# An audio tower on one core: two scale-and-add steps leave VectorE for ScalarE and GpSimd, and every engine's order is written anew

## The reference, cut to what matters

```python
h = tok(x)                                        # 32 x 626 x 128: frames of 128 samples times a DCT basis
h = h + mamba_both_ways(layernorm(h))             # L0_attn
h = h + experts(layernorm(h))                     # L0_ffn: 8 experts, the best 2 for each token
h = h + attention(layernorm(h))                   # L1_attn
h = h + patterns(layernorm(h))                    # L1_ffn: top 64 of 512, top 128 of 256, top 64 of 512

# in L0_attn, for each direction: y is the scan's output, gated
y = y * silu(z)
y = y * rsqrt(mean(y * y, -1) + EPS) * normw
y @ Wout.T                                        # both directions are projected, added to x and normalised
# in L0_ffn
combined = einsum('td,te->td', expert_out, gate_output)     # two experts' answers, each times its weight
```

## Time and profile before

| | |
|---|---|
| median of 3 runs | 8031.15 us (7994.39 to 8032.64) |
| profiled execution, its own time | 8044.3 us |
| its span, first to last instruction | 8042.4 us |
| mean granted TensorE clock | 0.867 of full speed |
| busy: PE, DVE, ACT, POOL | 76%, 84%, 45%, 31% |

### The profile page before, as it was taken

One profiled execution on the slowest core, in us unless ns is written; L12 is line 12 of the kernel. 1 busy time (PEld: TensorE's weight loads), 2 busy tenths in 40 slices (PEclk: granted clock), 3 DMA queues, 4 the chain that ended last, 5 costly groups with the idle time before them and its releaser, 6 DMA issues.

```text
span 8042.4 us, 115198 instructions
## 1 busy us (share of the span) xinstructions
PE 6126.0 (76%) x34088; PEld 4811.3 (60%) x34088; DVE 6747.5 (84%) x21836; ACT 3593.5 (45%) x7726; POOL 2468.3 (31%) x2872
## 2 busy tenths in 40 slices
PE   6777787877787777777777778777778777778643
PEld 5656666656666656666656666666666666666422
DVE  2368889888888888889888889888988888888897
ACT  2344445444445444445444445444445444445321
POOL 2233332233332233332233332323332333332220
PEclk8888898888888888898888899888889888889766
DMA  2322222222222222222222222221222222222200
GB/s 71 112 72 67 67 86 78 66 68 67 67 86 78 66 69 65 66 86 79 65 72 65 66 84 79 72 71 59 66 82 79 75 69 63 64 81 80 68 6 4
DMA packets 342571, 560.36 MB, mean 70 GB/s; under 512 B 33728, under 2 KB 261792, under 8 KB 341664
## 3 DMA queue, kind: packets, MB, share of 16 engines
q10 hardware_dynamic: 152576, 357.68, 14.1%
q1 hardware_dynamic: 168992, 153.83, 7.0%
q0 software_dynamic: 20480, 41.98, 1.8%
HBM read 484.63 MB, written 68.74 MB: 69 GB/s over the span
## 4 chain that ended last, share of the span: by engine, by line
PE 36%; DVE 27%; ACT 15%; issue 10%; POOL 6%; ACTq 4%; DMA 2%; POOLq 0%; DVEq 0%; SPq 0%
DVE m L1230 6%; PE pM L656 6%; PE pS L547 5%; PE pM L667 4%; PE pA L709 4%; DVE work L1233 3%; POOL rows L449 3%; DVE sorted L1260 2%; DVE work L1263 2%; ACT hid L915 2%; DVE a L1233 2%; ACTq L895 2%; PE pS L609 2%; PE pS L601 2%; PE pA L721 2%
## 5 line engine op out<-in xcount | busy, mean ns | idle before, releaser
L1230 DVE MAX8 m<-work 128x8 f32<-128x512 f32 x1792 | 1143.6, 680 | 1.0
L547 PE MATMUL pS<-u_fm,wconv_s 128*128 128x315 f32 x3072 | 1015.0, 485 | 94.1 <-ACT xs L860 87.0
L1233 DVE MATCH_REPLACE8 work<-m,work 128x512 f32<-128x512 f32 x1536 | 1026.6, 676 | 0.0
L656 PE MATMUL pM<-turned,expert 128*128 128x128 f32 x4352 | 675.3, 304 | 409.5 <-ACT turned L928 399.2
L410 POOL TENSOR_TENSOR yg<-xs,zs 128x525 f32<-128x525 f32 (+1 forms) x256 | 195.9, 797 | 2489.8 <-ACT xs L870 2489.8
L656 PEld LDWEIGHTS pM<-turned,expert 128*128 128x128 f32 x4352 | 606.2, 213 | 522.5 <-issue 492.5
L547 PEld LDWEIGHTS pS<-u_fm,wconv_s 128*128 128x128 f32 x3072 | 654.0, 217 | 404.6 <-issue 128.3
L915 ACT ACTIVATE hid<-pM,expert 128x128 f32<-128x128 f32 x2176 | 623.2, 372 | 250.5 <-PE pM L656 249.0
L1230 DVE MAX8 m<-a 128x8 f32<-128x512 f32 x768 | 505.4, 679 | 187.9 <-issue 180.9
L667 PE MATMUL pM<-expert,hid 128*128 128x128 f32 x4352 | 629.1, 292 | 0.0
L1263 DVE MATCH_REPLACE8 work<-sorted,work 128x128 f32<-128x128 f32 x2240 | 591.6, 276 | 0.0
(11 more groups left out here) (255 smaller groups left out, 14526.7 us busy)
## 6 DMA issues: line engine op xcount, KB each, us to landing
expert<-in_experts ACTq DMA_DIRECT2D x544, 578.0 KB, 4.0
ab<-decay_rows SPq DMA_DIRECT2D x384, 230.7 KB
rows<-routed_rows SPq DMA_DIRECT2D x128, 256.0 KB, 3.6
answer_rows<-turned ACTq DMA_DIRECT2D x256, 128.0 KB, 3.9
x_sb<-in_x SPq DMA_DIRECT2D x32, 256.0 KB
out<-hk SPq DMA_DIRECT2D x32, 256.0 KB
routed_rows<-un,slot POOLq DMA_INDIRECT x320, 2.2
rows<-answer_rows,slot POOLq DMA_INDIRECT x320, 2.6
```

Source lines behind the costliest of these rows:

```text
L547: last = nc.tensor.matmul(pS[:, 512 * (n % 3):512 * (n % 3) + HQ], wt, tap(d, i, half * HQ, HQ), start=(j == 0), stop=(j == len(blocks) - 1))
L656: last = nc.tensor.matmul(pM[:, bank(i) + j * P:bank(i) + (j + 1) * P], w1_of(i, j), turned[:, (i + 2) % 4, 1, :], start=True, stop=True)
L1230: link(nc.vector.max(m8[:, i, :], now[i]), len(tiles) - 1)
L1233: link(nc.vector.match_replace(work[i], m8[:, i, :], now[i], GONE), len(tiles) - 1)
```

## The change

Two pieces of VectorE's work are done elsewhere, and the five order strings are new.

- The scaled scan outputs. Ten instructions on DVE (multiply and add) become ten on ACT (a copy out of PSUM with a scale for each partition, into the first half of `zs4`, `dir_out`) and two adds of 128x640 on POOL.
- The experts' answers. Ten instructions on DVE become ten on ACT (scaling `rows` in place, `scaled`) and two adds of 128x640 on POOL (`h3_part`, `moe_done`).

```diff
-    o_ps=1, ub=1, r_norm=1, attn_scaled=2, h1_done=1,
+    o_ps=1, ub=3, dir_out=1, r_norm=1, attn_scaled=2, h1_done=1,
...
-DVE_ORDER = ("342414424142141142444444444414414444141114111441111111411114111414444444341444414444444344344344342")
+DVE_ORDER = ("44432414422141211444444444444434444411144114314434444134444111131111411111114441144444144444444441")
...
@@ pool_stage1
+            pool.wait_ge(G["dir_out"].s, G["dir_out"](b, 1))
+            for d in range(2):
+                pool.wait_ge(G["ub"].s, G["ub"](b, d + 1))
+                nc.gpsimd.tensor_tensor(ub[:], ub[:], zs4[:, d, 0, :].rearrange("p (t d) -> p t d", t=TILES), ALU.add).then_inc(G["ub"].s, 1)
+            yield
             normalized(pool, 0, 3, b, u, ub).then_inc(G["r_norm"].s, 1)
...
@@ pool_stage2
+            pool.wait_ge(G["scaled"].s, G["scaled"](b, 1))
+            pool.wait_ge(G["h3_kept"].s, G["h3_kept"](b, 0))
+            pool.wait_ge(G["u4_done"].s, G["u4_done"](b, 0))
+            nc.gpsimd.tensor_tensor(h3[:], h2[:], rows[:, 0:TILES, :], ALU.add).then_inc(G["h3_part"].s, 1)
+            pool.wait_ge(G["h3_part"].s, G["h3_part"](b, 1))
+            nc.gpsimd.tensor_tensor(h3[:], h3[:], rows[:, TILES:, :], ALU.add).then_inc(G["moe_done"].s, 1)
...
@@ act_stage1
+            act.wait_ge(G["o_ps"].s, G["o_ps"](b, 1))
+            act.wait_ge(G["rstd1"].s, G["rstd1"](b, 2))
+            for k in range(2 * TILES):
+                d, t = divmod(k, TILES)
+                last = nc.scalar.activation(zs4[:, d, 0, tok(t)], pS[:, tok(k)], ACT.Copy, scale=rstd[0][:, k:k + 1])
+            last.then_inc(G["dir_out"].s, 1)
...
@@ act_stage2
+            act.wait_ge(gathered.s, gathered(b, 160))
+            for k in range(2 * TILES):
+                last = nc.scalar.activation(rows[:, k, :], rows[:, k, :], ACT.Copy, scale=top8[:, k % TILES, k // TILES:k // TILES + 1])
+            last.then_inc(G["scaled"].s, 1)
...
@@ dve_stage1
-            for d in range(2):
-                for t in range(TILES):
-                    k = d * TILES + t
-                    last = nc.vector.scalar_tensor_tensor(ub[:, t, :], pS[:, tok(k)], rstd[0][:, k:k + 1], ub[:, t, :], ALU.mult, ALU.add)
-                link(last)
+            dve.wait_ge(G["ub"].s, G["ub"](b, 3))
             moments(link, 0, ub, G["var1"])
...
@@ dve_stage2
-            for t in range(TILES):
-                last = nc.vector.scalar_tensor_tensor(h3[:, t, :], rows[:, t, :], top8[:, t, 0:1], h2[:, t, :], ALU.mult, ALU.add)
-            link(last)
-            for t in range(TILES):
-                last = nc.vector.scalar_tensor_tensor(h3[:, t, :], rows[:, TILES + t, :], top8[:, t, 1:2], h3[:, t, :], ALU.mult, ALU.add)
-            last.then_inc(G["moe_done"].s, 1)
```

## The result

The changed kernel takes 7719.9 us (median of 4 runs, 7710.2 to 7727.2), the kernel before 8031.9 us on the same chip: a ratio of 0.9616, 95% interval 0.9579 to 0.9653. The direction was right, the size was not: 312 us gained and not 110.

A forecast was written before the change was run, and what follows sets the result against it. DVE was taken as nearly the bound, 209.9 of 239.0 us a round. Work and gaps 207.2 plus waits 28.0 make 235.2 us, 3.8 less; over 29 rounds 110 us, so 7920 us, range 7720 to 8080.

The forecast's parts named there:

- What bounds the kernel: One 239.0 us round: DVE nearly the bound, 209.9 us of work, 26.2 of named waits, 2.9 of gaps.
- What is removed and added: DVE loses 5.57 us a round; ACT gets 2.7 us per ten copies, POOL 3.1 us per pair of adds.
- The boundary, 16.1 us: Round's end: a 32.9 us chain of power, copies, five finishes and `a1` leaves DVE waiting 16.1 us, 10.0 before.
- so I take the slow price: Five finishes at the round's end: PE at half clock, so each repeats every 4.65 us, 22.05 us in all.
- The chain to `o_ps`, 2.0 us: From the last weigh but one: PE's chain takes 27 us, DVE's way 25.0, so DVE waits 2.0 us.
- rival 3: Slower: the PE chain from last weigh to `o_ps` runs long, 39 us; round 244, time 8170; chance 0.21.
- The other waits: DVE's remaining waits in a round, at L1252, L1099, L1230 and small new places: 8.4 us together.
- L1252's wait stays, 5.5 us: DVE's wait for ACT's last a2 stays 5.5 us, as ACT's work from first selection to there is the same.
- The small ones: New short DVE waits: 1.0 us before the reciprocal, 0.6 before L1277's scans, 0.5 behind the router's exponential.
- The port lock: Stage 1's first scans on DVE can be held by POOL's products through the shared port: 1.5 us a round.
- Prologue and epilogue, left as they are: Three rounds before the loop, three after: no net change; hand-overs cost some 3 us, DVE work saves 2.8.
- Rival 1: PE's clock stays up at the round's end: finishes 3.06 us apart, round 226.5, time 7670; chance 0.20.

The follow-up runs named there:

- order_only: The new order strings with the code of the kernel before, so all moved work stays on DVE: 7925.7 us, ratio 0.9672 to the kernel before.
- fill_first: The changed kernel with 12 extra 128x128 products on PE behind the first finish's transposes: 7663.7 us, ratio 0.9566 to the kernel before.
- act_swap: The changed kernel with ACT's ten scaled scan-output copies behind the first finish's copy, not ahead: 7814.7 us, ratio 0.9552 to the kernel before.
- scan_dve: The changed kernel with only the scan outputs' scaling and adding given back to DVE: 7841.7 us, ratio 0.9574 to the kernel before.
- fill: The changed kernel with extra PE products, 18 in the first finish and 2 in each other: 7906.3 us, ratio 0.9662 to the kernel before.
- pool_swap: The changed kernel with POOL's two adds to `ub` ahead of its ten gathers, not behind: 7920.8 us, ratio 0.9687 to the kernel before.
- moves_only: The order strings of before, adjusted only to place the moved work, with the changed kernel's code: 8359.2 us, ratio 1.0191 to the kernel before.

## Why the prediction was wrong, step by step

- **What bounds the kernel.** Right that the waits decide. The round of before was taken as 239.0 us from one pair of rows; over the loop it is 240.4. That is 1.4 us a round, 41 us in all.
- **What is removed and added.** The prices held: ten scaled copies took 2.69 us out of PSUM and 3.03 on `rows` (2.7), POOL's adds 1.53 to 1.58 each. The step "5.57 us a round" off DVE held as work, and was worth nothing as time on the chips where it was tried: `order_only` keeps that work and is as fast.
- **The boundary, 16.1 us.** The first MAX8 waits 10.6 us in the mean and `ub` 3.3, 13.9 together. In the two rounds whose finishes were slow to the end it is 15.0 and 16.3, which is the forecast; in the other two the clock rose on the way, and it is 10.6 and 13.6. So the chain as I drew it was right at half clock, and what failed is the step "so I take the slow price" for all five finishes. `fill_first` shows that the clock sets the price, `act_swap` and `scan_dve` that this chain (power, copies, finishes) is the path. What I did not see is the next link: the fourth finish can't start before DVE's own selection ends. PE waits 0.7 to 2.9 us for it in the four kernels whose chain was shortened, and `fill_first`, `scan_dve` and `act_swap` gained 2.4 to 3.6 us a round.
- **The chain to `o_ps`, 2.0 us.** Measured 0.15 (0.6 us once in four rounds). In the round with the wait the chain took 25.6 us (4101.16 to 4126.76) and not 27, and DVE's way 25.0, as counted. PE did start slowly (clock 0.81 from 4103 to 4107 us), but 3 us was too much for it, and rival 3 did not come. It was near, though: without the register load DVE waits 3.0 us there. Rival 3 also has a slip: 12 us beyond 27 make a round of 247 us and a time of about 8270, not 244 and 8170.
- **The other waits: this step failed most.** "L1252's wait stays, 5.5 us" became 1.9:

```profile
3929.57 0.56 DVE L1252 TENSOR_TENSOR work<-a 128x384 f32<-128x384 f32 x1 [5.48 <-ACT a L987]
...
3996.02 0.56 DVE L1259 TENSOR_TENSOR work<-a 128x384 f32<-128x384 f32 x1 [1.87 <-ACT a L1012]
```

  ACT's chain from DVE's first MAX8 to the last a2 of the first three tiles is as long as before (67.7 us, 3861.76 to 3929.47, and 67.5 after, 3928.44 to 3995.91). But DVE comes to its own wait 65.7 us after that MAX8 where it came after 62.3: of the 3.4 us, 2.2 are work that the new string puts ahead (63.2 us busy on the way and not 61.0) and 1.1 are the small waits at L1158 and L1091. I priced the chain and not DVE's way to it. That the chain is equal is luck: its register load became 1.9 us shorter (4.4 and 2.5 us), which I had not expected, and the rest of it 1.7 longer. The step costs 3.6 us a round, 104 us in all, the largest single term. This is read from the traces; no run changed DVE's way alone.
- **The small ones.** L1124 1.0 (0.4), the reciprocal 0.7 (1.0), the router 0.3 (0.5), L1277's scans 0 (0.6), 0.6 at the third selection's first MAX8 (0.4), and 0.8 at L1091 that I had at nothing.
- **The port lock.** 1.5 us forecast. The mean of L1116 is 1308 ns where L1091's was 1168: 12 x 0.14 = 1.7 us a round. It is the orders' doing, since `order_only` has 1321 ns.
- **Prologue and epilogue, left as they are.** They cost 35 us more. `order_only` has the same long third round ahead of the loop (199.2 us, and 182.0 before), so most of this too is the orders'.

The waits are 6.8 us less than forecast, the work 0.2 less, and the round of before 1.4 more: with rounding 8.3 us, which is the step from 3.8 to 12.1 a round. Rival 1 (the clock stays up) came true in part, in two of the four rounds.

## What to carry to other kernels

When work leaves the busiest engine and the orders change in the same step, cost the two apart: the moved work is worth only what the engine does not then wait. Here it was all given back as waits, while the orders alone made the gain, and it paid 1.2% only when the order was fitted to it (`act_swap`). A kept wait has two sides; compute when the waiting engine gets there as carefully as when the other delivers. Take a round from the whole loop, not from one pair of rows, and after shortening a chain look for the link that was waiting just behind it: here two digits in ACT's order gave 1.3% more, and then PE waited for DVE's own selection.

## What the runs showed of the hardware

- The same register loads on ACT, in the same program, took 2.5 us on one chip and 5.5 to 6.1 on another, and the rows behind them came 3 to 4 us later. In another order of the same pieces they took 4.4 us on a chip of either kind. The time of the kernel before differs by 2% between such chips; how much of that is these loads is open.
- A scan of DVE that normally takes 1.17 us took 2.15 at 4041.8 us, while POOL's L483 ran (4037.34 to 4042.94). The first row below is the changed kernel's scans in 960 us (minimum, median, maximum ns), the second before's, where none was long:

```profile
L1116 DVE TENSOR_TENSOR_SCAN ab<-ab,cst x56: 1149/1170/2150, 3612.6 to 4545.7; 121x488 f32<-121x488 f32 x56
...
L1091 DVE TENSOR_TENSOR_SCAN ab<-ab,cst x48: 1162/1168/1177, 3683.9 to 4463.9; 121x488 f32<-121x488 f32 x48
```

  The Trainium skill, "SBUF — State Buffer", section "SBUF: two separate sides", calls the shared port pair an exclusive lock for the whole instruction; by that rule, the trace agrees.
- In four rounds each of `fill`, `pool_swap` and `moves_only`, ten copies on ACT within a finish waited 3.3 to 6.6 us, released by "remote", while POOL issued its ten gathers: 3772.99, 4007.65, 4242.46 and 4479.36 us in `fill`, 4017.72, 4251.87 and 4487.36 in `pool_swap`, 3770.36, 4021.23 and 4272.97 in `moves_only`. POOL's last gather ended at 3773.05, 4006.34, 4241.23 and 4479.59; 4017.86, 4250.52 and 4486.02; 3769.21, 4021.55 and 4271.77. All lie within 1.4 us of it. The other kernels issue the same gathers and show no such wait. What holds the copy was not tried and stays open; so does how much of `moves_only`'s loss it makes.
